# Three of sixteen columns selected by TensorE, thirteen gathered by GpSimd

## The reference

```
h = relu(layernorm(x))                                  # (12500, 32)
e = concat([h[src], h[dst], edge_attr], axis=-1)        # (412500, 96)
v = relu(e @ W1 + b1) @ W2 + b2                         # (412500, 32)
x_cand = segment_max(v, dst, num_segments=12500)
out = x + maximum(x_cand, h)
```

## Time and profile before

| | |
|---|---|
| median of 3 runs | 3732.7 us (3724.38 to 3733.32) |
| profiled execution | 3732.61 us |
| its span | 3730.8 us |
| mean granted clock of TensorE | 0.883 |
| gathers by GpSimd | 2,821 |
| matmuls of `select` | 5,642 |

### The profile page before, as it was taken

One profiled execution on the slowest core, in us unless ns is written; L12 is line 12 of the kernel. 1 busy time (PEld: TensorE's weight loads), 2 busy tenths in 40 slices (PEclk: granted clock), 3 DMA queues, 4 the chain that ended last, 5 costly groups with the idle time before them and its releaser, 6 DMA issues.

```text
span 3730.8 us, 43135 instructions
## 1 busy us (share of the span) xinstructions
PE 2795.1 (75%) x11492; PEld 1936.0 (52%) x11492; DVE 2097.5 (56%) x3562; ACT 761.6 (20%) x1058; POOL 2735.6 (73%) x2852
## 2 busy tenths in 40 slices
PE   2488877777787788787877777877877778778776
PEld 1365555555555555555555555555555555555554
DVE  7365555555555555555555555555555555555555
ACT  5022122112121212121121212211212212112111
POOL 5277777777777777777777777777777777777774
PEclk9698888898898889888988988989889889889888
DMA  5422222222222222222222223233233333223321
GB/s 145 107 69 63 70 66 63 68 67 65 67 65 67 66 61 70 67 62 67 67 65 66 67 65 65 65 64 68 63 66 68 64 65 68 66 63 64 70 60 29
DMA packets 245710, 253.28 MB, mean 68 GB/s; under 512 B 83264, under 2 KB 199478, under 8 KB 239112
## 3 DMA queue, kind: packets, MB, share of 16 engines
q10 hardware_dynamic: 20790, 103.55, 11.2%
q1 hardware_dynamic: 133938, 101.54, 10.3%
q0 software_dynamic: 90784, 46.48, 8.2%
HBM read 239.86 MB, written 11.52 MB: 67 GB/s over the span
## 4 chain that ended last, share of the span: by engine, by line
POOL 67%; issue 22%; PE 3%; DVE 3%; SPq 2%; DMA 1%; POOLq 1%; ACT 0%; DVEq 0%
POOL feat L499 67%; PE ps_spare L589 1%; DMA feat<-h_rows,idx 1%; SPq L321 1%; DVE feat_t L899 1%; PE ps_hid L599 0%; DMA dst_rows<-key_rows 0%; PE ps_picked L631 0%; POOLq L487 0%; PE ps_hid L601 0%; PE ps_val L610 0%; DVE feat L1088 0%; SPq L288 0%; PE ps_spare L577 0%; SPq L320 0%
## 5 line engine op out<-in xcount | busy, mean ns | idle before, releaser
L499 POOL DMA_INDIRECT feat<-h_rows,idx x2821 | 2718.8, 964 | 950.7 <-issue 856.0
L589 PE MATMUL ps_spare<-table,key_hot 128*128 128x448 f32 x5642 | 1262.8, 380 | 23.5 <-DVE key_hot L963 23.5
L589 PEld LDWEIGHTS ps_spare<-table,key_hot 128*128 128x128 f32 x5642 | 1062.2, 188 | 201.3 <-issue 119.5
L556 PE MATMUL ps_feat<-ident,feat 128*128 128x128 f32 x806 | 188.4, 323 | 778.1 <-DMA feat<-h_rows,idx 778.1
L1011 DVE TENSOR_TENSOR best<-ps_picked,best 32x64 f32 x1612 | 355.6, 221 | 632.3 <-PE ps_picked L631 546.0
L556 PEld LDWEIGHTS ps_feat<-ident,feat 128*128 128x128 f32 x806 | 99.1, 156 | 826.8 <-DMA feat<-h_rows,idx 808.1
L599 PE MATMUL ps_hid<-feat_t,w_blk 128*128 128x512 f32 x806 | 474.7, 673 | 6.4 <-DVE edge_hot L956 6.0
L974 DVE SCALAR_TENSOR_TENSOR sel_tmp<-off_place,offset,ps_spare 128x448 f32<-128x448 f32 x403 | 272.4, 676 | 309.6 <-PE ps_spare L589 309.4
L963 DVE TENSOR_TENSOR key_hot<-dst_rows,ps_iota 128x1792 fp32r<-128x1792 f32 x202 | 406.1, 2011 | 44.5 <-DMA dst_rows<-key_rows 44.5
L601 PE MATMUL ps_hid<-edge_hot,term_ring 128*128 128x512 f32 x806 | 413.5, 595 | 0.0
L757 ACT COPY feat_t<-ps_feat 64x512 f32<-64x512 f32 x404 | 234.4, 580 | 862.8 <-PE ps_feat L556 860.5
(11 more groups left out here) (122 smaller groups left out, 816.7 us busy)
## 6 DMA issues: line engine op xcount, KB each, us to landing
dst_rows<-loc_rows ACTq DMA_DIRECT2D x98, 512.0 KB
feat_t<-attr_rows_in ACTq DMA_DIRECT2D x98, 512.0 KB
feat<-h_rows,idx POOLq DMA_INDIRECT x2821, 3.3
dst_rows<-key_rows SPq DMA_DIRECT2D x101, 256.0 KB, 6.1
term_ring<-term_rows SPq DMA_DIRECT2D x404, 64.0 KB
dst_rows<-keep_rows SPq DMA_DIRECT2D x100, 256.0 KB
term_rows<-best SPq DMA_DIRECT2D x3, 1792.0 KB
idx<-src_cols_in SPq DMA_DIRECT2D x51, 32.0 KB, 1.7
```

Source lines behind the costliest of these rows:

```text
L499: nc.gpsimd.indirect_dma_start(feat[:, slot, k, :], None, h_dram, bass.IndirectOffsetOnAxis(ap=idx[:, c % IDX, k:k + 1].bitcast(U32), axis=0),
L556: mm = pe.transpose(ps_feat[:, to:to + P], feat[:, slot, Q * b:Q * b + Q, :].rearrange("p q d -> p (q d)"), ident[:])
L589: mm = pe.matmul(ps_sel[c % TWO], key_hot[:, c // TWO % 2, g, P * (c % TWO):P * (c % TWO) + P], table[half][:, g, :], start=(g == 0 and ha ...
```

## The change

In a pair, the last column of the first chunk and the last two of the second are now selected by TensorE, and GpSimd gathers the other thirteen. `key_hot` becomes a ring of four one-hots, one for each column, and VectorE makes the next one straight behind each column that it has taken. TensorE does one of the three selections between `turn_features` and `pick_ends`, the other two at the end of the step as before. Key rows are loaded six at a time, and there are 606 of them where there were 408. `key_ring` gets a tile of its own, `term_ring` goes where it was, and the tiles in which keys are prepared lie over `x_even`, so that their loads wait until `x_even` was read.

```diff
-GK = COLS - 1
+SEL = 3
+HOTS = 4
...
-        key_hot = sb("key_hot", [P, 2, SG, TWO * P], F32R)
+        key_hot = sb("key_hot", [P, HOTS, SG, P], F32R)
+        key_ring = sb("key_ring", [P, 4 * SEL, P])
...
+        def gathered(c):
+
+            return COLS - 1 - c % TWO
+
+        def is_column(i, j):
+
+            return not known(i) or j < SEL * (NP - 1) + 1
+
+        def column(j):
+
+            n = j % SEL
+            return TWO * (j // SEL) + min(n, 1), COLS - 1 - n // 2
...
             def load_key(s, half):
-                sp.dma_start(key_ring[:, FOUR * half:FOUR * half + FOUR, :].rearrange("p c e -> p (c e)"),
-                             key_dram[bass.ds(s, FOUR), :].rearrange("c e -> (c e)").unsqueeze(0)
-                             .broadcast_to([P, FOUR * P])).then_inc(s_key[half], 16)
+                lo, n = half * 2 * SEL, 2 * SEL
+                sp.dma_start(key_ring[:, lo:lo + n, :].rearrange("p c e -> p (c e)"),
+                             key_dram[bass.ds(s, n), :].rearrange("c e -> (c e)").unsqueeze(0)
+                             .broadcast_to([P, n * P])).then_inc(s_key[half], 16)
...
+            sp.wait_ge(S["cent_done"], 2)
             sp.wait_ge(S["key_pad"], 1)
...
-                for k in range(GK):
+                for k in range(gathered(c)):
                     if c >= TWO * LEAD or not known(i):
-                        follow(i, c // TWO - LEAD, c % TWO * GK + k)
+                        follow(i, c // TWO - LEAD, c % TWO * gathered(0) + k)
...
             def turn_features(i, v):
                 n = wide(i, v)
-                pe.wait_ge(S["sel_ready"], i * UNROLL + TWO * v + n)
+                pe.wait_ge(S["sel_ready"], i * (SEL * UP) + (SEL * v + (SEL if n > 1 else 1)))
...
-            def select(i, c):
-                pe.wait_ge(S["hots_made"], i * UP + c // TWO + 1)
-                if not known(i) or c >= TWO:
-                    pe.wait_ge(S["sel_step"], i * UNROLL + c - 1)
+            def select(i, j):
+                pe.wait_ge(S["hots_made"], i * (SEL * UP) + j + 1)
+                if not known(i) or j > 1:
+                    pe.wait_ge(S["sel_step"], i * (SEL * UP) + j - 1)
...
             def step(i, v):
+                ahead = [j for j in range(SEL * v + 2 * SEL - 1, SEL * v + 3 * SEL - 1) if is_column(i, j)]
                 if later(i, v - 1):
                     turn_ends(i, v - 2)
                 turn_features(i, v)
+                for j in ahead[0:1]:
+                    select(i, j)
                 if later(i, v - 1):
                     pick_ends(i, v - 2)
                 if later(i, v):
                     second_layer(i, v - 1)
                 first_layer(i, v)
-                for c in range(TWO * v + 2 * TWO, TWO * v + 3 * TWO):
-                    if is_chunk(i, c):
-                        select(i, c)
+                for j in ahead[1:3]:
+                    select(i, j)
...
-            def place_keys(i, v):
...
+            def place_keys(i, j):
...
                 nc.vector.tensor_tensor(
-                    key_hot[:, v % 2, :, :],
-                    key_ring[:, slot:slot + TWO, :].rearrange("p c e -> p (c e)").unsqueeze(1)
-                    .broadcast_to([P, SG, TWO * P]),
-                    key_place.unsqueeze(2).broadcast_to([P, SG, TWO * P]),
+                    key_hot[:, j % HOTS, :, :],
+                    key_ring[:, j % (4 * SEL), :].unsqueeze(1).broadcast_to([P, SG, P]),
+                    key_place.unsqueeze(2).broadcast_to([P, SG, P]),
                     ALU.is_equal).then_inc(S["hots_made"], 1)
...
+                if is_column(i, j + HOTS):
+                    place_keys(i, j + HOTS)
...
             def step(i, v):
+                ahead = [j for j in range(SEL * v + SEL, SEL * v + 2 * SEL) if is_column(i, j)]
...
                 place_edges(i, v)
-                if is_chunk(i, TWO * v + 2):
-                    take_selected(i, TWO * v + 2)
+                for j in ahead[0:1]:
+                    take_selected(i, j)
                 if later(i, v - 1):
                     split_ends(i, v - 2)
-                if is_chunk(i, TWO * v + 3):
-                    take_selected(i, TWO * v + 3)
-                if is_chunk(i, TWO * v + 6):
-                    place_keys(i, v + 3)
+                for j in ahead[1:2]:
+                    take_selected(i, j)
                 if later(i, v - 1):
                     keep_best(i, v - 2)
+                for j in ahead[2:3]:
+                    take_selected(i, j)
```

More of the change, by code:

```diff
@@ L163, in gnn_layer @@
         keep_ring = shared[:, LOCS:LOCS + KEEPS].bitcast(BF16).rearrange("p (r n) -> p r n", n=2 * P)
-        key_ring = shared[:, LOCS + KEEPS:LOCS + 2 * KEEPS].bitcast(F32).rearrange("p (r e) -> p r e", e=P)
+        term_ring = shared[:, LOCS + KEEPS:LOCS + 2 * KEEPS].bitcast(F32).rearrange("p (r e) -> p r e", e=P)
+        spare = x_even[:].rearrange("p t d -> p (t d)")
+        key_stage = spare[:, 0:NSB * P].rearrange("p (b e) -> p b e", e=P)
+        key_src = spare[:, NSB * P:2 * NSB * P].bitcast(I32).rearrange("p (b e) -> p b e", e=P)
+        off_src = spare[:, 2 * NSB * P:2 * NSB * P + NSEL].bitcast(I32)
+        off_key = spare[:, 2 * NSB * P + NSEL:2 * NSB * P + 2 * NSEL]
         any_dst = loc_ring[0:1, 0:2, :].rearrange("p r e -> p (r e)").bitcast(I32)
@@ L222, in gnn_layer @@
         LOOPS = (NP - PRE) // UP
-        TURN = 16 * GK
         def known(s):
@@ L350, in _ @@
                                  dst[LAST:E].rearrange("(r e) -> r e", r=1)).then_inc(S["dst_in"], 16)
-            full = CPAD // P
+            full = NSEL // P
+            sp.wait_ge(S["cent_done"], 2)
             sp.wait_ge(S["key_pad"], 1)
@@ L368, in _ @@
             sp.wait_ge(S["key_made"], 1)
-            for b in range(-(-CPAD // P)):
-                r = min(P, CPAD - b * P)
+            for b in range(NSB):
+                r = min(P, NSEL - b * P)
                 sp.dma_start(key_dram[b * P:b * P + r, :], key_stage[0:r, b, :]).then_inc(S["key_out"], 16)
@@ L581, in _ @@
                     turn_h(g + 2)
-            def select(i, c):
-                pe.wait_ge(S["hots_made"], i * UP + c // TWO + 1)
-                if not known(i) or c >= TWO:
-                    pe.wait_ge(S["sel_step"], i * UNROLL + c - 1)
+            def select(i, j):
+                pe.wait_ge(S["hots_made"], i * (SEL * UP) + j + 1)
+                if not known(i) or j > 1:
+                    pe.wait_ge(S["sel_step"], i * (SEL * UP) + j - 1)
                 for g in range(SG):
                     for half in range(2):
-                        mm = pe.matmul(ps_sel[c % TWO], key_hot[:, c // TWO % 2, g, P * (c % TWO):P * (c % TWO) + P],
-                                       table[half][:, g, :], start=(g == 0 and half == 0),
-                                       stop=(g == SG - 1 and half == 1))
+                        mm = pe.matmul(ps_sel[j % 2], key_hot[:, j % HOTS, g, :], table[half][:, g, :],
+                                       start=(g == 0 and half == 0), stop=(g == SG - 1 and half == 1))
                 mm.then_inc(S["sel_sum"], 1)
@@ L655, in _ @@
             pe.wait_ge(S["table_ready"], 2)
-            for c in range(2 * TWO):
-                select(0, c)
+            for j in range(2 * SEL - 1):
+                select(0, j)
             steps(pe, step, {1: turn_worst})
@@ L1045, in _ @@
             dve.wait_ge(S["firsts_in"], 16)
-            for v in range(2):
-                place_keys(0, v)
-            for c in range(TWO):
-                take_selected(0, c)
-            place_keys(0, 2)
+            for j in range(HOTS):
+                place_keys(0, j)
+            for j in range(SEL):
+                take_selected(0, j)
             steps(dve, step, {1: check})
@@ L1114 @@
     given["attr_rows"] = by_feature.reshape(-1, len(begins) * 4 * P)
-    picked = np.stack([np.asarray(src)[a:a + CE].reshape(2, P, Q)[1, :, Q - 1] for a in padded])
+    blocks = [np.asarray(src)[a:a + CE].reshape(2, P, Q)[1] for a in padded[0:len(begins) + len(begins) % 2]]
+    picked = np.stack([block[:, q] for n in range(0, len(blocks), 2)
+                       for block, q in ((blocks[n], Q - 1), (blocks[n + 1], Q - 1), (blocks[n + 1], Q - 2))])
     given["sel_rows"], given["sel_cols"] = picked, picked.T
```

59 lines of the change are left out of this document (29 added, 30 removed).

## The result

The changed kernel takes 3,462.9 us (median of 4 runs, 3,459.9 to 3,466.9), beside 3,730.2 for the kernel before: a ratio of 0.929 with a 95% interval of 0.9279 to 0.9301. The direction and the bound were as forecast; the time lies 27 us under the 3,490 predicted and 4 us under the lower end of the range. The profiled execution took 3,459.9 us, with a span of 3,458.1.

A forecast was written before the change was run, and what follows sets the result against it. GpSimd's gathers were taken as the bound: 3,732.6 - 246.0 (fewer gathers) + 1.0 (key preparation) + 1.5 (third key load) = 3,489, with a little for a later TensorE at the end 3,490 us; range 3,467 to 3,545.

The forecast's parts named there:

- GpSimd bounds the kernel, before and after, at 1.2485 us a gather: Main loop: GpSimd's gathers stay the bound; 197 steps fewer at 1.2485 us give -246.0 us.
- The 45.5 us beside `edge_hot` stay.: GpSimd's gathers in the main loop: time above 1.2485 us a step, some 0.23 us a pair, stays at 45.5 us.
- Rival C: GpSimd's gathers: their phase against `edge_hot` changes; if overlaps vanish, the 45.5 us go too, giving 3,445 us; chance 0.04.
- That load [...] adds between 0 and 9 us; I take 1.5.: Start of the main loop: the third key load, half as large again, adds 0 to 9 us, taken as 1.5.
- TensorE is hidden: Main loop: 14 more matmuls bring TensorE to 15.25 us a pair, under GpSimd's 16.46, leaving 1.2 us of cover.
- The new block fills the wait of the picks: TensorE between transposes and `pick_ends`: the added selection fills time in which `pick_ends` waits for the split ends.
- The bank wait: The new block's wait for VectorE's first taken column: 3 us to spare, so no wait expected.
- VectorE: Main loop: `key_hot` takes 1.07 us and VectorE 2.5 us more a pair, 12.5 in all, hidden under 16.46.
- Clock: TensorE's granted clock was to rise to 0.95 or more; staying at 0.88 would show the forecast wrong.
- Rival B: TensorE runs each pair's first part at 1.2 GHz although its waits are short, giving 3,861 us, slower; chance 0.03.
- Waits for gathers: TensorE's waits for GpSimd's gathers, the mean of 1.04 and 7.29 us a pair, fall to 1 to 1.5.
- Share of GpSimd on the chain: Sign that the forecast is right: GpSimd on 85 to 90% of the chain of work, 67% before the change.

The follow-up runs named there:

- the two kernels with the other `edge_hot`: One-hot of edges made by comparing two tensors instead of with a scalar: 3,429.0 us in the changed kernel, 3,687.1 us in the kernel before.
- the short block: The changed kernel with the middle selection of a pair cut from 14 matmuls to 2, leaving out part of the work: 3,479.2 us.

## Why the prediction was right, and where it was wrong

*GpSimd bounds the kernel, before and after, at 1.2485 us a gather.* Right. 197 steps fewer are the 246.0 us of the sum. Taken bare, in the two kernels with the other `edge_hot`, the steps themselves take 3,450.6 and 3,205.0 us, 245.5 apart.

*"The 45.5 us beside `edge_hot` stay."* Wrong in size, and the first of the two steps that failed: they were 30.2 us. The cause was named rightly, that a gather is longer beside `edge_hot`, but I took the loss per pair for a constant. It depends on where within a gather `edge_hot` begins. That this place is set by what VectorE waits for is my reading, from the runs side by side: where TensorE waits for gathers in most pairs, the excess was 40 to 46 us (the kernel before and its variants, and the short block); where it doesn't, 30 to 35. Rival C had the right mechanism, a third of its size, and only 0.04.

*"That load [...] adds between 0 and 9 us; I take 1.5."* Wrong in sign, the second step: the restart came 11.1 us earlier than before, not 2.5 later. I had taken the 17.8 us of the key load for a property of the load and asked what more bytes add. It was one of its neighbourhood: the added selections delay TensorE in step 1, hence ScalarE's load of the places, and the key load gets past it. The bounds excluded a gain without a reason.

Together these are 15.3 + 13.6 us, and with either alone the time would have been within the range.

*TensorE is hidden.* Right: 15.06 us against 15.25 predicted. With the short block its 18% of the chain are gone and the time isn't lower. The cover was thin as said, and thinner for another order of the same instructions.

*The new block fills the wait of the picks.* Right, in the trace (no wait between 1,289.19 and 1,292.09); without it the pair is 1.2 us longer, which would still just have been hidden. What would not is a third block at the end.

*The bank wait.* Right: the group of `select` shows no wait for `sel_tmp` in the main loop. *VectorE:* `key_hot` takes 1.077 us (1.07 predicted), 12.1 us a pair (12.5). *Clock:* a mean of 0.97, from 0.883, as predicted. Rival B fell as to the time, but not for its reason: "short waits keep the clock" was too wide. Between 300 and 3,400 us the granted clock still falls to 0.50 in 42 stretches, most of 3.4 us and 150 us in all, each around the end of a wait for gathers of 1.97 to 2.97 us (in the kernel before 116 stretches, 703 us). So the rule that B named (the Trainium skill, TensorE: Matmul & The Clock Gate, A second HAM failure mode: psum-queue depth-cycling) does show: the clock goes up and down all through the loop. It costs nothing here, since TensorE waits in these very pairs. *Waits for gathers:* 161 us in all, 0.8 a pair, a little under the 1 to 1.5 predicted, and none over 3.0. *Share of GpSimd on the chain:* 49% where I wrote 85 to 90%; a wrong sign to look for, since two engines that keep nearly the same pace share the chain without sharing the blame.

Left open: why the key load takes 17.8 us beside the places in the kernel before and 18.2 in the one with the short block, but only 9.2 and 11.4 when the places are put ahead of it in two variants of the changed kernel. The order and the spacing to the places and to the masks differ there, and no run separates them. Also open is by which waits the change moved `edge_hot` within a gather: the table shows where it went, not why.

## What to carry to other kernels

A bound engine's step has a bare part and a part that neighbours add. The second depends on when the neighbours run, so it doesn't carry over to a kernel whose other engines wait for something else; give it a range from nothing to what it could be, and look for another form of the instruction that causes it, even a slower one. How long a load in the head takes can be a question of what is issued just ahead of it on any queue, so ask which engine's delay reorders those issues. And when work moves to an engine with little room left, its place in the step decides: with the same 42 matmuls of selection a pair cost TensorE 15.1, 16.2 or 17.3 us.

## What the runs showed of the hardware

- An indirect DMA of 128 rows cost GpSimd 1.2485 us, within 0.0001 us in two kernels; a VectorE `tensor_scalar` (bf16 in, fp32 out, some 0.75 us) beside it stretched it by up to 0.5 us, a `tensor_tensor` of the same elements with one operand in PSUM (1.21 us) not at all.
- The Trainium skill (SBUF — State Buffer, Who interferes with whom) has the one that comes second blocked for as long as the first one's instruction lasts. The rows agree: a gather with `edge_hot` begun 0.24 to 0.40 us in ended some 0.12 us behind it. But the loss was not the 0.75 us of that instruction. It was on average 0.23 us a pair in the kernel before and 0.15 in the changed one, and next to nothing where `edge_hot` was over early in the gather.
- Leaving out 12 of 42 matmuls a pair made the kernel 16 us slower.
- The third key load took 7.5 to 8.9 us where the load of the places came 2.8 us or more behind it, and 15.5 to 18.2 us where the places went out 0.7 to 1.3 us ahead of it and the masks ahead of those; with both 0.6 us ahead it took 11.4.
- TensorE's granted clock fell to 0.50 around the end of waits of 1.97 to 2.97 us, 42 times in the changed kernel; a block of 14 matmuls then took 4.64 us instead of 3.07.
- Once in eight pairs VectorE stood for 1.3 to 1.7 us of "issue" ahead of its scan. Where the picks waited for VectorE and no pair waited for gathers, that and the lower clock made such a pair 18.3 to 21.3 us long instead of some 17.
